# The activations' transposes in a mixture-of-experts kernel: from TensorE with a PSUM copy to two DMA transposes per slot

## What is computed

```python
probs = jax.nn.softmax(x @ gate_w.T, axis=-1)
vals, idx = jax.lax.top_k(probs, K)                    # K = 4 of E = 16
w = vals / jnp.sum(vals, axis=-1, keepdims=True)
combine = jnp.einsum('tke,tk->te', jax.nn.one_hot(idx, E, dtype=x.dtype), w)
act = swiglu(jnp.einsum('th,ehi->eti', x, w_gu))       # silu(gate) * up
y_e = jnp.einsum('eti,eih->eth', act, w_d)
out = jnp.einsum('te,eth->th', combine, y_e)
act_s = swiglu(x @ dequant_fp4(shared_gate_up_packed, shared_gate_up_scales))
out = out + act_s @ dequant_fp4(shared_down_packed, shared_down_scales)
```

## Time and profile before

| what | value |
|---|---|
| median of 3 runs | 693.31 us (694.84, 693.31, 689.36) |
| span of the profiled execution | 689.3 us; no other time of it is listed |
| TensorE busy | 622.6 us, 90% |
| VectorE, ScalarE, GpSimd busy | 496.2, 325.8, 327.7 us |
| DMA moved | 93.72 MB, mean 136 GB/s |

### The profile page before, as it was taken

The page is one execution under the profiler, slowest core; times in us unless marked ns, Lnnn a source line. Parts: engine busy times, 40 slices in busy tenths (PEclk is TensorE's granted clock), DMA queues, the critical chain, the costliest instruction groups (busy, mean ns, idle before and its releaser), DMA issues.

```text
span 689.3 us, 17258 instructions
## 1 busy us (share of the span) xinstructions
PE 622.6 (90%) x4394; PEld 375.9 (55%) x4395; DVE 496.2 (72%) x1271; ACT 325.8 (47%) x558; POOL 327.7 (48%) x506
## 2 busy tenths in 40 slices
PE   3668869887898999999999999999999999999992
PEld 2444545444554656565555656566565655656550
DVE  5878788989776858588777867688588878867210
ACT  1763577231343554454544455454554545455441
POOL 2521844000235456564646565564655656565432
PEclk9999989998999999999999999999999999999996
DMA  8670111128156875857577684848767587654432
GB/s 235 203 241 1 63 46 70 40 53 276 49 162 152 207 179 118 189 115 189 107 196 174 128 215 82 225 78 204 177 127 186 117 193 174 141 89 68 90 47 31
DMA packets 49841, 93.72 MB, mean 136 GB/s; under 512 B 8840, under 2 KB 16776, under 8 KB 49816
## 3 DMA queue, kind: packets, MB, share of 16 engines
q0 software_dynamic: 16128, 38.35, 30.1%
q1 hardware_dynamic: 32936, 55.04, 27.1%
q10 hardware_dynamic: 752, 0.04, 0.1%
HBM read 65.16 MB, written 28.24 MB: 135 GB/s over the span
## 4 chain that ended last, share of the span: by engine, by line
PE 72%; DVE 13%; ACT 4%; DMA 3%; issue 3%; POOL 2%; SPq 1%; DVEq 0%; POOLq 0%; ACTq 0%
PE gu_ps L1203 41%; PE bank L1231 20%; PE bank L1243 4%; PE bank L1217 4%; DVE mix_room L1023 2%; DMA dn_sc<-dn_scale_halves 2%; DVE act L989 1%; DMA room_a<-in_ctx 1%; ACT acth L620 1%; PE gu_ps L1163 1%; DVE X L998 1%; PE bank L1160 1%; DVE acth L994 1%; DVE dn_code L920 1%; ACT mix_room L579 1%
## 5 line engine op out<-in xcount | busy, mean ns | idle before, releaser
L1203 PE MATMUL gu_ps<-wgu,mix_room 128*128 x1728 | 304.4, 326 | 3.3 <-DVE tick L948 2.1
L1203 PEld LDWEIGHTS gu_ps<-wgu,mix_room 128*128 128x128 f16 x1728 | 166.0, 98 | 114.5 <-issue 7.4
L1231 PE MATMUL bank<-wdn,aT 128*128 (+1 forms) x792 | 186.5, 381 | 4.2 <-ACT aT L627 3.7
L528 POOL DMA_INDIRECT out<-mix_room,idx_s x72 | 123.9, 1721 | 31.9 <-issue 30.5
L627 ACT ACTIVATE aT<-bank 128x768 f16<-128x768 f16 x88 | 71.2, 810 | 130.9 <-PE bank L1217 126.0
L1231 PEld LDWEIGHTS bank<-wdn,aT 128*128 128x128 f16 x792 | 77.6, 98 | 89.5 <-issue 3.2
L989 DVE SCALAR_TENSOR_TENSOR act<-gu_ps,wslot,sg x72 | 44.5, 618 | 96.2 <-ACT sg L613 79.4
L499 POOL TENSOR_TENSOR pool_tick<-ones 128x1 f32<-128x1 f32 x144 | 36.0, 250 | 162.7 <-DMA out<-mix_room,idx_s 79.6
L620 ACT ACTIVATE acth<-act 128x384 f16<-128x384 f32 x88 | 46.0, 523 | 135.8 <-DVE act L989 131.4
L510 POOL DMA_INDIRECT room_b<-token_rows,idx_g x72 | 76.5, 1063 | 12.1 <-issue 3.7
L994 DVE TENSOR_TENSOR acth<-act,acth (+1 forms) x88 | 49.2, 560 | 38.1 <-ACT acth L620 37.6
(11 more groups left out here) (156 smaller groups left out, 586.2 us busy)
## 6 DMA issues: line engine op xcount, KB each, us to landing
dn_sc<-dn_scale_halves SPq DMA_DIRECT2D x34, 384.0 KB
dn_raw<-in_L_ffn_down_packed SPq DMA_DIRECT2D x48, 256.0 KB
gu_sc<-gu_scale_halves SPq DMA_DIRECT2D x34, 192.0 KB
X<-in_x SPq DMA_DIRECT2D x4, 1024.0 KB, 8.1
token_rows<-room_a SPq DMA_DIRECT2D x16, 256.0 KB, 2.3
out<-X SPq DMA_DIRECT2D x4, 1024.0 KB, 10.6
gu_raw<-in_L_ffn_gate_up_packed SPq DMA_DIRECT2D x16, 192.0 KB
gu_raw<-in_L_ffn_gate_up_packed SPq DMA_DIRECT2D x16, 191.9 KB
```

Of the source, the lines that this page charges most:

```text
L528: nc.gpsimd.indirect_dma_start(out[:, :], bass.IndirectOffsetOnAxis(idx_s[:, b:b + 1], 0), y_sb[:, b, :], None, compute_op=ALU.add).then_i ...
L1203: mm = nc.tensor.matmul(ps[b][:, 0:I], x(xp * HC + c), wgu[:, w, wp, c, col:col + I], start=(c == 0 and xp == 0 and wp == 0), stop=(c == H ...
L1231: mm = nc.tensor.matmul(y_ps[0 if shared else b][:, :], aT[:, b, ap, t, :], wdn[:, w, wp, t, :], start=(n == 0), stop=(n == 3 * IC - 1))
```

## The change

`transpose_act` and `copy_aT` are gone, and the PSUM bank `at_ps` with them. A new step of ScalarE, `turn`, follows `high_halves` in the same slot: it waits for the high part and issues a DMA transpose of `acth[:, b, 0]` (128x384) straight into `aT[:, b, 0]`, then waits for VectorE's low part and issues one for that. Each has a semaphore per buffer set. `down` now waits for the high part's transfer, runs the six products that use it, waits for the low part's transfer, and runs the other three. The waits on `at_done` ahead of `activations` and `high_halves` are gone as well.

```diff
             def activate(s, b):
                 gate(s, b)
                 high_halves(s, b)
+                turn(s, b)
...
-            def copy_aT(s, b):
-
-                a.wait_ge(at_done, s + 1)
-                if not isinstance(s, int) or s >= 2:
-                    a.wait_ge(y_done, s - 1)
-                nc.scalar.activation(aT[:, b].rearrange("p a c t -> p (a c t)"), at_ps, ACT.Copy).then_inc(aT_done, 1)
+            def turn(s, b):
+
+                a.wait_ge(ah_done, s + 1)
+                a.sem_inc(act_held, 1)
+                a.dma_start_transpose(aT[:, b, 0], acth[:, b, 0, :]).then_inc(aTh_ld[b], 16)
+                a.wait_ge(al_done, s + 1)
+                a.sem_inc(act_held, 1)
+                a.dma_start_transpose(aT[:, b, 1], acth[:, b, 1, :]).then_inc(aTl_ld[b], 16)
...
-            def transpose_act(s, b):
-                pe.wait_ge(ah_done, s + 1)
-                pe.wait_ge(al_done, s + 1)
-                if not isinstance(s, int) or s >= 1:
-                    pe.wait_ge(aT_done, s)
-                for hl in range(2):
-                    for t in range(IC):
-                        k = hl * IC + t
-                        mm = nc.tensor.transpose(at_ps[:, k * P:(k + 1) * P], acth[:, b, hl, t * P:(t + 1) * P], id16[:, :])
-                mm.then_inc(at_done, 1)
-
             def down(s, b, w):
-                pe.wait_ge(aT_done, s + 1)
+                pe.wait_ge(aTh_ld[b], 8 * (s - b) + 16)
...
-                for t in range(IC):
-                    for ap, wp in ((0, 0), (0, 1), (1, 0)):
+                for t, ap, wp in [(t, 0, wp) for t in range(IC) for wp in range(2)] + [(t, 1, 0) for t in range(IC)]:
+                        if n == 2 * IC:
+                            pe.wait_ge(aTl_ld[b], 8 * (s - b) + 16)
                         mm = nc.tensor.matmul(y_ps[0 if shared else b][:, :], aT[:, b, ap, t, :], wdn[:, w, wp, t, :],
```

More of the change, by code:

```diff
@@ L215, in gated_xattn_moe @@
         g_ps, u_ps = bank[0:2], bank[2:4]
-        at_ps = bank[4][:, 0:IC * P].bitcast(F16)
         y_ps = bank[5:7]
@@ L265, in gated_xattn_moe @@
         al_done = sem("al_done")
-        at_done = sem("at_done")
-        aT_done = sem("aT_done")
+        aTh_ld = [sem("aTh_ld0"), sem("aTh_ld1")]
+        aTl_ld = [sem("aTl_ld0"), sem("aTl_ld1")]
+        act_held = sem("act_held")
         y_done = sem("y_done")
@@ L617, in high_halves @@
                 a.wait_ge(act_done, s + 1)
-                if not isinstance(s, int) or s >= 2:
-                    a.wait_ge(at_done, s - 1)
                 nc.scalar.activation(acth[:, b, 0, :], act[:, b, :], ACT.Copy).then_inc(ah_done, 1)
-            def copy_aT(s, b):
-                a.wait_ge(at_done, s + 1)
-                if not isinstance(s, int) or s >= 2:
-                    a.wait_ge(y_done, s - 1)
-                nc.scalar.activation(aT[:, b].rearrange("p a c t -> p (a c t)"), at_ps, ACT.Copy).then_inc(aT_done, 1)
+            def turn(s, b):
[5 more added lines that the diff above has]
+                a.dma_start_transpose(aT[:, b, 1], acth[:, b, 1, :]).then_inc(aTl_ld[b], 16)
             def take_rows(r, b):
@@ L648, in _ @@
                 activate(i, i)
-            copy_aT(0, 0)
             for i in range(2, NT):
-                copy_aT(i - 1, (i - 1) % 2)
                 if i in WITH_X:
@@ L676, in slot @@
             def slot(r, b, rows=True):
-                copy_aT(r + (NT - 1), 1 - b)
                 if rows:
@@ L689, in _ @@
             slot(2 * inner + 3, 1, rows=False)
-            copy_aT(2 * inner + 3 + NT, 1)
             take_y(2 * inner + 3, 1)
@@ L984, in activations @@
             def activations(s, b, weight):
-                if not isinstance(s, int) or s >= 2:
-                    v.wait_ge(at_done, s - 1)
                 v.wait_ge(sg_done, s + 1)
@@ L1276, in _ @@
             route(TB - 1)
-            transpose_act(0, 0)
             for i in range(2, NT):
@@ L1285, in _ @@
                     down(0, 0, 0)
-                transpose_act(i - 1, 1 - b)
                 if i in WITH_X:
@@ L1320, in slot @@
                 gate_up(s, b, x, w, 0)
-                transpose_act(s - 1, 1 - b)
                 if rows:
@@ L1338, in _ @@
             slot(2 * inner + 3, 1, rows=False)
-            transpose_act(2 * inner + 3 + NT, 1)
             e_last = pe.value_load(slot_i[0:1, bass.ds(2 * inner + 3, 1)], min_val=0, max_val=E - 1)
```

## The result

The changed kernel takes 839.7 us (median of four executions, 835.0 to 846.1), beside 691.3 us for the kernel before on the same chip: 1.215 times as long, 95% interval 1.209 to 1.220. The forecast was 712 us with a range to 800. The direction was right; the time lies above the range.

A forecast was written before the change was run, and what follows sets the result against it. The prediction took TensorE's own stream to bound the kernel. From 689.3 us, 29.2 for transposes leaving and plus 47.6 for late landings gave 707.7; 4.0 more for the median made 712 us, range 660 to 800.

The forecast's parts named there:

- What TensorE gives back: Six transposes per slot leave TensorE's stream, 0.34 us each slot: 24.5 us routed, 4.7 shared, together 29.2 us.
- ScalarE's issue: Two DMA issues per routed slot on ScalarE's queue, 1.06 us each, beside 4.10 us already there: 6.22 of 6.28, costing nothing.
- The landing: Second-stage products wait for DMA data: hidden in quiet stretches, late beside weight loads, 47.6 us in all, bounds 0 and 95.
- The size of one lateness: In loaded stretches a high part lands after 7.3 us, where 3.91 are available: 3.4 us late.
- The count: One late landing per expert weight load, 14 in the routed stage, each 3.4 us.
- the argument that the next slot's transfer has had the time of the wait: After a late slot shifts TensorE by 3.4 us, the next slot's activation has that much more time and fits.
- the transfer's own load: The transposes' 192 KB per slot add about 0.13 to the DMA share; smaller pieces would make it more.
- the last rival: Many small transpose pieces fill the DMA engines, or an issue costs over 1.74 us: above 800 us, chance 0.09.
- a rival of its own: Late starts lower TensorE's granted clock, 17 to 88 us more: 729 to 800 us, chance 0.20 shared with ScalarE's queue.
- which waits would show it: Second-stage products held by the transposes' landing in loaded stretches alone, some 3 us at a time.
- The tail: At the end, the chain from L620's end to the products goes from 2.4 to 2.3 us: nothing.
- a hidden landing: Rival: transposes land within 3.91 us even beside weight loads; 660 to 664 us, up to 686, chance 0.34.

The follow-up runs named there:

- e3: The changed kernel without any transposition: no DMA transposes, no waits on them, a constant in aT; 664.5 us, ratio 0.963.
- e7: As e3, with about 1.2 us of dummy ScalarE work in place of each transpose issue, and no transfer; 687.7 us, ratio 0.995.
- e2: The changed kernel with the weight and scale loads of the last 14 experts cut to 16 columns; 743.8 us, ratio 1.078.
- e11: The changed kernel with one whole-slot transpose per slot, second-stage products one slot later, GpSimd's gathers moved back against the scatters; 821.8 us, ratio 1.190.
- e1: The changed kernel with plain DMA copies of the same bytes in place of the two transposes per slot; 754.0 us, ratio 1.092.
- e5: As e1, with aT padded so that the plain copies fall into pieces of 256 bytes; 804.8 us, ratio 1.166.
- e14: As e11, with one plain copy of both parts per slot in place of the transpose; 698.5 us, ratio 1.013.
- e12: As e11, with a DMA transpose of the low part alone and a constant for the high part; 741.5 us, ratio 1.073.
- e10: The kernel before, transposes still on TensorE, with its six high-part products ahead of its three low-part ones; 690.9 us, ratio 1.000.

## Why the prediction was wrong

**What TensorE gives back** was taken at 29.2 us; e3 lies 25.9 under the span of before. The routed slots gave 27.8 in place of 24.5 us, the shared ones nothing in place of 4.7: scaling by the busy share there was a mistake, since that stage has waits that the time saved falls into (those for `room_a` are 17.0 us before and 20.9 in e3).

**ScalarE's issue** was taken at 1.06 us, between 0.45 and 1.74; it is 1.20. That is past the 1.09 from which the forecast let ScalarE set the pace, and short of the 1.26 of a loss. By the forecast's own formula a slot is 4.10 + 2 x 1.20 = 6.50 us; in e7 it is 459.3 / 71 = 6.47. So the price was a little low, 9.1 us, and the sum fits. That ScalarE's queue sets this pace is not shown: from 240 to 670 us of e7 TensorE is busy 421.34 of 430 us, and the waits listed for it there are for gathered rows (8.4 us). What the forecast did not have are the 14.6 us ahead of the routed slots, where ScalarE's queue holds what stands behind the two issues, the preparation of `room_a` among it; e7, with the same time and no transfer, shows the loss.

**The landing** is the step that failed: 47.6 us in the forecast, with a bound of 95, and 152 in the runs (839.7 - 687.7). Three parts of that step were wrong.
- The size of one lateness. With nothing beside it a transpose lands in 2.3 us, as forecast, and a wait in the loaded stretches is 3.8 us in the mean, near the 3.4 of the forecast. But the 7.3 us of the earlier trace rows for a loaded landing, taken from one 32 KB load, was not an upper bound: 11.3 and 13.5 us occur.
- The count, above all. The forecast had one excess per weight load, 14 in all, and in every other slot a landing as in a quiet place. There are 39 waits. By the packets in the trace, 21 of them (79.8 us) ended on a transpose beside which the loads moved some 600 pieces or more; the other 18 (37.8 us, 2.1 in the mean) on one beside which they moved 64 at most, in 11 cases none, so that GpSimd's gathers and scatters alone made it late, as at 512.16. e2, with the loads of 14 experts cut, keeps 35 waits. And the argument that the next slot's transfer has had the time of the wait fails by e11: in a loaded stretch the transfers of successive slots queue up, so a later start of the products doesn't let the transfer catch up.
- What it was taken for. The forecast set the transfer's own load at 0.13 of the DMA engines "if its pieces are as large" and left "small pieces would make it more" without a price. The pieces are of 237 bytes, and their number costs 50.7 us at equal bytes (e1 to e5). The mechanism stood in the last rival, a transpose of many small pieces, over 800 us, at a chance of 0.09; but the 89.5 us of plain copies over no transfer (e3 to e1) are more than the number of pieces costs.

Why a transfer is so late beside others stays open. One picture, an estimate worked out from rows, is that the engines serve the queues in turn, piece by piece. From the page of the kernel after a piece takes 0.155 x 16 x 839.3 / 73,968 us = 28 ns on ScalarE's queue, 102 on SyncE's, 236 on GpSimd's. Over 16 engines 416 pieces are 26 turns, 0.7 us with no other queue busy and 9.5 beside both; the 800 pieces of a whole slot need 18, near the 17 us of e11. It does not come out for plain copies. Their 144 pieces are 9 turns, 3.4 us at 35 ns a piece in e1, and their landings, of e1 (low part) and of e14, reach 8.5 and 8.6 us:

```profile
DMA to landing us min/median/max: 1.9/2.9/8.5
```

```profile
DMA to landing us min/median/max: 2.1/3.5/8.6
```

By the packets in the traces, the first piece of a transfer beside the loads moves 3.4 us after its issue in the median of e14 and 3.9 in e12, and after 1.2 us or less with nothing beside it. That part of the lateness does not come from the transfer's own pieces. The Trainium skill, page DMA: Bandwidth & Descriptors, section Queues, rings and completion order, has the engines go round between the queues, a packet at a time, and has several descriptors in a packet; no run here shows the turns themselves, nor whether a piece of the profile is such a packet.

Where a transfer is late, the loss doesn't stay with it: the same TensorE instructions take 51.7 us longer than in e3, at a granted clock of 0.91 in the mean against 0.97, and 0.76 after the wait shown. The forecast had this as a rival of its own (729 to 800 us, that is 17 to 88 us more); it came with the landing, not in its place, and the 45.3 us over e7 lie inside that price. VectorE's unpacking and the copy of y wait behind the same products.

Right were the free order of the products (e10), that the low part's wait on ScalarE lies inside the first issue (528.15 + 1.20, then 529.46), and which waits would show it, though not that they would stand in the loaded stretches alone. The tail was put at nothing: from the last copy of y to the end it is 10.9 us before and 11.0 after, but the chain ahead of that copy, from the end of the high part (820.23) to the products (824.60), is 4.4 us, where the forecast had 2.3. The rule that the prediction had as favouring a hidden landing, that transposing DMAs are as fast as plain ones (the Trainium skill, Advanced Engine Details and Errata, section X-Bar Transpose (TRN2)), does not hold for this kernel: 839.7 us against 754.0 for plain copies of the same tiles.

No kernel that does all the work beat the one before, and the runs point to none: with all six transposes off TensorE and nothing in their place the most there is to gain is 26 us, and the two issues alone take 23 of it. A slot's high part by TensorE and low part by DMA was not tried, nor the transposes on a queue other than ScalarE's.

## What to carry to other kernels

Before a small step moves from TensorE to DMA, count the pieces it falls into and look at what else the DMA engines carry in the stretch where its result is awaited, gathers and scatters as well as loads; bytes and a quiet latency don't tell. Price a wait in a loaded stretch as a rate (does the transfer keep up with the slots?), not as one lateness. And price the issue on the queue that makes it in every stage, also where its engine looks idle by its busy share.

## What was not expected of the hardware

- A DMA transpose of 128x384 float16 from SBUF to SBUF goes in 416 packets of 237 bytes; a plain copy of the same tile goes in 144 of 683 bytes. The transpose's issue takes ScalarE 1.20 us, and 1.23 us at twice the size; a plain copy's takes 0.47 us, and 0.60 in 256-byte pieces.
- By the packets in the trace of the kernel after, from 220 us on, the transposes whose landing it gives take 2.3 us in the median with nothing beside them (15 transfers), 5.3 beside GpSimd's gathers and scatters alone (20), and 10.0 beside the weight loads (25).
- In the loaded stretches the mean DMA share reads 1.20 at 238 GB/s, and 1.26 at 149 GB/s in e11: a share of 1 is not the limit of that view.
